# Triangular inverse of layers 2 and 3: the transposes of steps 1 to 4 made by VectorE in 32x32 blocks in place of TensorE

## The reference

```python
A0 = jnp.tril(-(jnp.einsum('bhnid,bhnjd->bhnij', k_beta, k) * L[None, :, None]), -1)
M = eye - A0
A = solve_triangular(M, jnp.broadcast_to(eye, M.shape), lower=True, unit_diagonal=True)
v = A @ v
k_cumdecay = A @ (k_beta * decay_exp)
def step(S, inp):
    k_i, v_i, kcd_i = inp
    attn = jnp.tril(jnp.einsum('bhid,bhjd->bhij', k_i, k_i) * L[None])
    v_new = v_i - kcd_i @ S
    o_i = k_i * de @ S + attn @ v_new
    S_new = chunk_total_decay * S + jnp.einsum('bhcd,bhce->bhde', k_i * dw, v_new)
    return (S_new, o_i)
```

```python
def step(S, inp):
    q_t, k_t, v_t, a_t, b_t = inp
    a = a_t[:, :, None]
    b = b_t[:, :, None]
    Sk = jnp.einsum('bij,bj->bi', S, k_t)
    S = a * (S - b * (Sk[:, :, None] * k_t[:, None, :])) + b * (v_t[:, :, None] * k_t[:, None, :])
    o = jnp.einsum('bi,bij->bj', q_t, S)
    return (S, o)
```

## Time and profile before

| | us |
|---|---|
| median of 3 runs (1846.14 to 1849.55) | 1847.09 |
| span of the profiled execution | 1846.0 |
| lowest of the three runs | 1846.14 |

### The profile page before, as it was taken

The page is one execution under the profiler, slowest core; times in us unless marked ns, Lnnn a source line. Parts: engine busy times, 40 slices in busy tenths (PEclk is TensorE's granted clock), DMA queues, the critical chain, the costliest instruction groups (busy, mean ns, idle before and its releaser), DMA issues.

```text
span 1846.0 us, 31832 instructions
## 1 busy us (share of the span) xinstructions
PE 1761.5 (95%) x10270; PEld 1337.9 (72%) x10270; DVE 1318.2 (71%) x4547; ACT 1083.0 (59%) x2686; POOL 1177.9 (64%) x1539
## 2 busy tenths in 40 slices
PE   7999999989999999999999999999998999999988
PEld 5788988756576666666666667777887887888874
DVE  7864256698879887988889775546557756678683
ACT  5554236555676577777775785446544556544555
POOL 5565568887878777868778864134437664444456
PEclk9999999999999999999999999999999999999999
DMA  6100000010000000000000000000000010000002
GB/s 239 64 24 1 1 4 1 3 48 1 1 2 1 1 1 1 1 1 1 1 1 1 1 10 5 1 1 8 2 1 2 3 29 17 20 1 1 2 7 63
DMA packets 24473, 26.44 MB, mean 14 GB/s; under 512 B 3492, under 2 KB 21284, under 8 KB 23924
## 3 DMA queue, kind: packets, MB, share of 16 engines
q1 hardware_dynamic: 24308, 24.41, 4.1%
HBM read 22.26 MB, written 2.15 MB: 13 GB/s over the span
## 4 chain that ended last, share of the span: by engine, by line
PE 75%; DVE 12%; ACT 4%; POOL 4%; issue 3%; DMA 1%; SPq 0%; POOLq 0%; DVEq 0%; ACTq 0%
PE ps L86 69%; PE ps L89 6%; POOL arena L103 4%; DVE arena L103 4%; ACT arena L97 3%; DVE arena L106 2%; DVE arena L141 2%; DVE arena L109 1%; DVE arena L126 1%; ACT L97 1%; DVE arena L129 1%; DMA cst<-in_cst 0%; DVE arena L123 0%; SPq L146 0%; DVE arena L132 0%
## 5 line engine op out<-in xcount | busy, mean ns | idle before, releaser
L103 POOL TENSOR_TENSOR arena<-arena 128x128 f32<-128x128 f32 (+6 forms) x796 | 694.3, 885 | 354.4 <-DVE arena L109 126.1
L97 ACT ACTIVATE arena<-ps 128x128 f32<-128x128 f32 (+13 forms) x1100 | 352.7, 354 | 448.2 <-PE ps L86 316.2
L86 PE MATMUL ps<-arena 128*128 128x128 f32 (+4 forms) x2864 | 462.7, 296 | 26.4 <-DVE arena L103 18.1
L86 PEld LDWEIGHTS ps<-arena 128*128 128x128 f32 x2864 | 382.0, 192 | 129.2 <-issue 62.7
L103 DVE TENSOR_TENSOR arena<-ps,arena 128x128 f32<-128x128 f32 (+4 forms) x680 | 313.9, 474 | 164.2 <-PE ps L86 150.5
L97 ACT ACTIVATE arena<-arena 128x128 f32<-128x128 f32 (+1 forms) x772 | 300.0, 442 | 37.5 <-POOL arena L103 27.8
L97 ACT ACTIVATE arena<-ps,cols 128x512 f32<-128x512 f32 x324 | 218.1, 688 | 172.3 <-PE ps L86 157.2
L86 PE MATMUL ps<-arena,cst 128*128 128x504 f32 (+2 forms) x768 | 289.2, 494 | 10.1 <-DVE arena L103 4.1
L86 PE MATMUL ps<-arena,moe 128*128 128x256 f32 (+1 forms) x960 | 289.1, 440 | 1.0 <-DVE arena L103 0.4
L89 PE MATMUL ps<-cst,arena 128*128 128x128 f32 (+1 forms) x1392 | 238.5, 275 | 17.6 <-ACT arena L97 6.3
L103 POOL TENSOR_TENSOR arena<-arena,cst 128x144 f32<-128x144 f32 (+7 forms) x320 | 139.9, 440 | 146.8 <-ACT arena L97 84.8
(11 more groups left out here) (109 smaller groups left out, 1876.2 us busy)
## 6 DMA issues: line engine op xcount, KB each, us to landing
rows<-in_rows SPq DMA_DIRECT2D x1, 2253.0 KB, 15.5
arena<-in_x SPq DMA_DIRECT2D x8, 256.0 KB, 5.3
wf<-in_wf SPq DMA_DIRECT2D x2, 1024.0 KB, 6.0
arena<-in_L_ffn_W SPq DMA_DIRECT2D x8, 256.0 KB, 2.9
out_dram<-arena SPq DMA_DIRECT2D x8, 256.0 KB, 2.7
wmod<-in_wmod SPq DMA_DIRECT2D x4, 384.0 KB, 7.8
arena<-kept SPq DMA_DIRECT2D x24, 64.0 KB, 2.9
arena<-kept SPq DMA_DIRECT2D x8, 192.0 KB, 3.2
```

Of the source, the lines that this page charges most:

```text
L86: return UNSENT if self.e is None else self.e.matmul(out, lhsT, rhs, start=start, stop=stop)
L97: return self.e.activation(out, in_, func, bias=bias, scale=scale)
L103: return UNSENT if self.e is None else self.e.tensor_tensor(out, a, c, op)
```

## The change

`BLOCKWISE` lists steps 1 to 4. In these, PE makes no transposes and takes no PSUM bank for them. DVE transposes M itself with one instruction that transposes each 32x32 block on its own, reading `G4` and writing `Y`, and then masks `Y` in place. All that the mask keeps in these steps lies in the diagonal 32x32 blocks, where a transpose by blocks and a full one agree. The `yield`s stand where they stood, so that `TURNS` selects the same places for everything else.

```diff
+    def tr32(self, out, a):
+        return UNSENT if self.e is None else self.e.transpose(out, a)
...
+        BLOCKWISE = (1, 2, 3, 4)
+
         def inv_pe(b, m, *key):
             for n in range(7):
-                ps = banks.take(pe, b, b, "inv_f", n, *key)
-                if n:
-                    pe.wait_ge(*at("inv_v", b, n, *key))
-                else:
-                    pe.wait_ge(*at("inv_m", b, *key))
-                for i in range(4):
-                    ins = pe.tr(ps[:, col4(i)], m.G4[:, i, 0:128] if n else m.tri[:, col4(i)], ident)
-                ins.then_inc(*pe.up(b, "inv_f", b, n, *key))
+                if n not in BLOCKWISE:
+                    ps = banks.take(pe, b, b, "inv_f", n, *key)
+                    if n:
+                        pe.wait_ge(*at("inv_v", b, n, *key))
+                    else:
+                        pe.wait_ge(*at("inv_m", b, *key))
+                    for i in range(4):
+                        ins = pe.tr(ps[:, col4(i)], m.G4[:, i, 0:128] if n else m.tri[:, col4(i)], ident)
+                    ins.then_inc(*pe.up(b, "inv_f", b, n, *key))
                 yield
                 ps = banks.take(pe, b, b, "inv_p", n, *key)
-                if n == 0:
-                    pe.wait_ge(*at("inv_v", b, 0, *key))
+                if n == 0 or n in BLOCKWISE:
+                    pe.wait_ge(*at("inv_v", b, n, *key))
                 pe.wait_ge(*at("inv_y", b, n, *key))
...
             for n in range(1, 7):
                 yield
-                ps = banks.get(b, "inv_f", n, *key)
-                dve.wait_ge(*at("inv_f", b, n, *key))
-                dve.tt(four(m.Y), four(ps[:, :]), over(neg(n)), ALU.mult).then_inc(
-                    *dve.up(b, "inv_y", b, n, *key, free=(b, "inv_f", n, *key)))
+                if n in BLOCKWISE:
+                    dve.wait_ge(*at("inv_p", b, n - 1, *key))
+                    dve.wait_ge(*at("inv_v", b, n, *key))
+                    dve.tr32(four(m.Y), m.M4).then_inc(*dve.up(b))
+                    dve.wait_ge(*dve.last(b))
+                    dve.tt(four(m.Y), four(m.Y), over(neg(n)), ALU.mult).then_inc(*dve.up(b, "inv_y", b, n, *key))
+                else:
+                    ps = banks.get(b, "inv_f", n, *key)
+                    dve.wait_ge(*at("inv_f", b, n, *key))
+                    dve.tt(four(m.Y), four(ps[:, :]), over(neg(n)), ALU.mult).then_inc(
+                        *dve.up(b, "inv_y", b, n, *key, free=(b, "inv_f", n, *key)))
```

## The result

The changed kernel is slower. Its median is 1869.07 us (1867.57 to 1869.97) against 1846.62 us for the kernel before on the same chip; the ratio is 1.0119, interval 1.0107 to 1.0131, which is 22 us. The forecast was 1840 with a range from 1825 to 1860: the sign was wrong, and the time lies outside the range. The profiled execution has a span of 1866.8 us, 20.8 more than before, and the inversions end at 1779 us where they ended at 1757. So the stretch of the inversions explains all of it.

A forecast was written before the change was run, and what follows sets the result against it. PE was taken as the bound. PE's 28 us less against DVE's 52 us more gave a gain of 2.9 us (10 us windows) to 10.7 (20 us); 7 us was taken, a median of 1840, range 1825 to 1860.

The forecast's parts named there:

- the relief: PE's queue in steps 1 to 4: 64 groups of four transposes removed, 0.44 us each, 28 us at most.
- So PE is the bound here: Inversions' stretch: PE busy 452.6 of 470 us and 80.2% of the chain; DVE has 147 us to spare.
- the busier of the two: Sum over windows of the busier of PE and DVE: gain 2.9 us (10 us windows) or 10.7 (20 us).
- Engines do lend each other that much: Load moves over borders of 10 us windows, so the gain lies between 2.9 and 10.7 us; 7 taken.
- What the step costs DVE: DVE's queue in steps 1 to 4: transpose 0.69 us, 0.81 us added a step, 52 us in all.
- the port: Mask multiplication reading SBUF twice, which can stand in POOL's way: 0.03 us a step in the sum.
- The latency of a step: From transposes through mask in one step: 1.33 us before, 1.44 after, said to hardly change.
- rival 2: Multiplications with two SBUF inputs wait for POOL: 0.94 us a step, about 1845, no change; chance 0.17.
- PSUM banks: Products in PE's order change bank with four takes fewer; costed at nothing.
- Rival 1: Packed stretches, above all 1600 to 1620: DVE becomes the bound, slower, about 1852 or 1872; break-even 0.88 or 1.09; chance 0.3.
- Rival 3: Steps 1 to 4: the whole relief arrives if DVE's transpose costs 0.46 us, about 1832; chance 0.1.
- The signs: Profile marks: transposes 0.6 to 0.8 us, DVE's waits a third, PE's waits up 15 to 20; wrong if masks exceed 0.85.

The follow-up runs named there:

- e5: Kernel before without anyone's transposes in steps 1 to 4; DVE masks the product in its PSUM bank, PE waits for ACT's copy first: 1839.74 us.
- e9: e5 with DVE's 64 transposes put back behind the multiplication, read by nobody: 1851.86 us.
- e6: Changed kernel, but DVE transposes into the product's PSUM bank and masks from there, and PE waits for ACT's copy before taking the bank: 1858.30 us.
- e1: Changed kernel, but PE waits for ACT's copy before it asks for the bank, instead of behind it: 1865.90 us.
- e3: Kernel before with DVE's 64 transposes added, each overwritten by the multiplication that still reads PE's transposes: 1861.16 us.
- e12: Changed kernel with an instruction's waits on the same semaphore merged into the one for the highest count: 1861.61 us.
- e10: Kernel before with an instruction's waits on the same semaphore merged into the one for the highest count: 1846.18 us.
- e2: Changed kernel with nobody transposing in steps 1 to 4; the multiplication reads untransposed `G4`, so two SBUF inputs: 1846.87 us.
- e4: Changed kernel with PE's transposes kept in their old places, unread: 1867.50 us.

## Why the prediction was wrong

| step added | kernel | us against before | this step |
|---|---|---|---|
| PE's transposes gone | e5 | -8.9 | -8.9 |
| DVE's transposes, off the chain | e9 | +3.0 | +11.9 |
| the transpose in the chain | e6 | +9.4 | +6.4 |
| both inputs of the mask from SBUF | e1 | +18.1 | +8.7 |
| fourth wait ahead of the product | after | +22.0 | +3.9 |

Three rows have a second measurement or a near one: the second e3 (+12.7 on its own), the fifth e12 (7.2, less e10's 2.4), and the fourth, less closely, e2 against e5 (7.8 with the fourth wait in it). The third was measured once. Single rows are uncertain by some 3 to 5 us each. The split also depends on the order in which the steps are added: the relief is worth 8.9 us as the first step and 9.7 between e3 and e9, but 0.4 as the last one (e4 against e1).

**The step that failed** is the first: "PE is busy for 452.6 of 470 us ... So PE is the bound here", and with it "the busier of the two" as a rule for the sum. The rule, fed with the relief alone, gives -25.5 us in windows of 10 and -26.5 in windows of 20; e5 measured -8.9. Busy time counted the tail of each record as work, so places with room in PE's queue looked full, which by the windows counted from starts explains 4 to 5 of the 17 us; and where an element's step is what others wait for, no engine is the bound at all, as from 1380 to 1480. For the load alone (0.81 us a step) the rule gives +11.4 and +5.8; e3 and e9 measured 12.7 and 11.9, so the finer windows were nearer, and "Engines do lend each other that much" was not borne out. By the table, relief and load together came to +3 where the forecast had -7, so this step is 10 of the 29 us between forecast and result; the other 19 are the three terms that follow, of which two had been put at nothing and one was too small.

**What the step costs DVE** was right: 0.69 us forecast for the transpose, 0.701 measured; 0.81 us of queue a step forecast, about 0.83 measured (0.70 less 0.08 for the transpose, 0.11 for the wait, 0.10 for the slower mask), with one part of it, the port, larger and none spent on other waits.

**The latency of a step** was said to go from 1.33 to 1.44 us, and the difference was not priced. By the means it is 0.70 + 0.03 + 0.79 = 1.52, and the transposes start 1.5 us behind ACT's copy on average, since they stand in line at DVE. From copy to product a step became 0.32 us longer, and it is this chain that sets the time where PE has room. e6 against e9 puts 6.4 us on it.

**The port** (rival 2) was the right mechanism with too small a price. The sum had 0.03 us for the second input, from the mean of 16 instructions; it was 0.10, or 6.4 us of DVE's queue, and up to 0.8 in single steps. POOL's side had no price; its 32-column masks became 0.07 us longer, and the product of the next step waits for one of them. Together 8.7 us of the kernel's time, where the rival gave a time of 1845. It was to show as a mean above 0.85 us; the mean was 0.77, and the cost came all the same.

**PSUM banks** were costed at nothing by asking which bank a product gets. What changed was the number of waits ahead of it: 3.9 us.

**Rival 1** (DVE becomes the bound) had the right sign by another route: a step came out at 0.83 us of DVE's queue, under the break-even of 0.88 that the rival gave. Its place was in part right: after 1600 DVE was full for 20 and 30 us at a time, but from 1380 to 1480, where over half of the time was lost, it was busy for 77 of 100. Rival 3, the whole relief, needed a transpose of 0.46 us; it took 0.70, and e5 excludes the relief itself. **The signs** that I named were nearly all seen as the forecast had them (the transpose at 0.70 us, the masks at 0.77 against a limit of 0.85, DVE's waits down to a third, PE's waits for multiplications up by 15.3 us), and the kernel was slower all the same. They tested the terms; the step that failed, what a relief of PE is worth, had no sign of its own.

What stays open: how the 11.9 us of load divide over the DVE instructions that were pushed back, how much of the loss after 1600 is a full DVE, why some meetings with POOL cost nothing, and whether an order of turns written for these lengths would win them back.

## What to carry to other kernels

Before you move work off the "full" engine, count its queue by the starts of its records and not by busy time, and look at stretches: gaps that overlap hides are room already there, and relief pays its full size only where they are absent. Even counted so, windows gave a relief of 20 to 23 us where 8.9 were measured. Load on an engine with spare time can cost once the chains of several elements run through it in a fixed order; price the relief alone and the load alone, each with an experiment of its own. Where POOL is busy on SBUF, try one input of DVE's two-input instructions in PSUM (8.7 us here), and don't wait twice on the same counter ahead of a matmul that others wait for.

## What the runs showed of the hardware

- DVE's transpose in 32x32 blocks, float32, 128x512, SBUF to SBUF: 701 ns (64 instructions, 681 to 712); into PSUM 716 ns.
- Where PE stands waiting, a matmul with three waits starts 0.10 us after its last operand's end, with a fourth wait 0.25 to 0.26 us; merging two of the four restores 0.10.
- A mask multiplication with both inputs in SBUF: 0.69 us in all 25 cases without a POOL instruction beside it and in 17 of the 39 with one; 0.94 to 1.49 in thirteen that started while POOL was running. With one input in PSUM 688 ns on average.
- PE's granted clock fell to half three times in the changed kernel's stretch (6.8, 3.4 and 3.4 us, from 1389.6, 1430.5 and 1488.6), each time within 1.3 us of the end of an idle stretch of PE (2.42, 1.41 and 0.79 us), and not once in the kernel before.
